# A two-layer sequence model on one core: the gates of chunks 1 to 3 a step ahead of their FFN, own orders for the first and last steps, parameters loaded first

## What is computed

```
x = layernorm(x + L0_attn(x))      # causal conv of 4 taps, gates r and i, recurrence, out projection, RMS norm
x = layernorm(x + relu(x @ W1 + b1) @ W2 + b2)
x = layernorm(x + L1_attn(x))      # selective state space, 16 states per channel
x = layernorm(x + relu(x @ w1 + b1) @ w2 + b2)

# L0_attn
xc = conv(x);  r = sigmoid(xc @ Wr.T + br);  i = sigmoid(xc @ Wi.T + bi)
a = sigmoid(log_a) ** (8 * r);  b = sqrt(clip(1 - a*a, 1e-6)) * (i * xc)
h[t] = a[t] * h[t-1] + b[t]        # with the log of the product of a clipped at -80
out = rmsnorm(h @ out_w.T) * norm_w
# L1_attn
xi, z = split(x @ in_proj.T);  xv = silu(conv(xi));  B, C, s = split(xv @ x_proj.T)
dt = softplus(s * dt_w + dt_b)
state[n][t] = exp(dt*A[n]) * state[n][t-1] + dt * B[n][t] * xv;  y = sum_n C[n][t] * state[n][t]
out = (y * silu(z)) @ out_proj.T
```

## Time and profile before

| | |
|---|---|
| median of 3 timed runs | 956.32 us (954.75 to 956.44) |
| the profiled execution, its own time | 953.83 us |
| its span in the profile | 952.0 us |
| busy: PE, DVE, ACT, POOL | 792.9, 786.3, 673.2, 586.6 us |
| mean granted clock of TensorE | 0.914 of 2.4 GHz |
| DMA | 19.49 MB, mean 20 GB/s |

### The profile page before, as it was taken

How to read it: one execution, slowest core, us unless ns; L and a number is a source line. 1 busy time by engine, 2 the same in 40 slices (tenths; PEclk the granted TensorE clock), 3 DMA queues, 4 the chain that set the end, 5 groups by cost and what they waited for, 6 DMA issues and landing times. The chain is left out here.

```text
span 952.0 us, 9608 instructions
## 1 busy us (share of the span) xinstructions
PE 792.9 (83%) x2802; PEld 530.0 (56%) x2802; DVE 786.3 (83%) x993; ACT 673.2 (71%) x1345; POOL 586.6 (62%) x488
## 2 busy tenths in 40 slices
PE   2285866988988899999999999998997797588685
PEld 2164643746565656475647564756475556356464
DVE  5425677486799999999999999999999999999750
ACT  4348687399768867997799779867976785474542
POOL 0203447448747786788678867886787577556431
PEclk9597977989998899999999999999999998799597
DMA  8100000000100010001000100010000000000000
...
DMA packets 10340, 19.49 MB, mean 20 GB/s; under 512 B 1456, under 2 KB 5296, under 8 KB 10288
## 3 DMA queue, kind: packets, MB, share of 16 engines
...
## 5 line engine op out<-in xcount | busy, mean ns | idle before, releaser
L384 POOL TENSOR_TENSOR y<-y,hC 128x1024 f32<-128x1024 f32 (+3 forms) x140 | 270.9, 1935 | 63.2 <-DVE hC L1475 58.9
L1916 PE MATMUL pC<-w,hT 128*128 128x256 f32 x1024 | 232.9, 382 | 4.4 <-ACT hT L777 4.3
L842 ACT ACTIVATE dA<-dt,A_neg 128x512 f32<-128x512 f32 (+3 forms) x320 | 185.6, 629 | 51.8 <-DVE hs L1464 51.6
L1916 PEld LDWEIGHTS pC<-w,hT 128*128 128x128 f32 x1024 | 193.5, 191 | 38.8 <-issue 6.3
L1464 DVE TENSOR_TENSOR_SCAN hs<-dA,carry,pS 128x512 f32<-128x512 f32 (+3 forms) x192 | 193.5, 1008 | 11.8 <-DVE pS L1449 4.0
L2039 PE MATMUL pS<-stack,sel 97*128 97x512 f32 (+3 forms) x320 | 151.7, 526 | 45.4 <-DVE hs L1464 45.3
L1449 DVE TENSOR_TENSOR pS<-u,pS 128x1024 f32<-128x1024 f32 (+3 forms) x160 | 159.6, 997 | 28.3 <-PE pS L2039 27.5
L1475 DVE TENSOR_TENSOR hC<-hs,pS 128x1024 f32<-128x1024 f32 (+3 forms) x160 | 158.0, 987 | 10.9 <-PE pS L2039 10.6
L1464 DVE TENSOR_TENSOR_SCAN hs<-dA,pS 128x512 f32<-128x512 f32 (+1 forms) x128 | 138.4, 1082 | 13.7 <-POOL carry L402 4.6
L777 ACT ACTIVATE hT<-pA,ffb_sb 128x512 f32<-128x512 f32 (+3 forms) x160 | 94.3, 597 | 64.0 <-PE pA L1909 63.7
L1909 PE MATMUL pA<-tg,w 128*128 128x512 f32 (+3 forms) x320 | 124.9, 538 | 5.2 <-ACT hT L777 4.8
...
## 6 DMA issues: line engine op xcount, KB each, us to landing
...
```

The costliest lines, as they stand in the source:

```text
L384: nc.gpsimd.tensor_tensor(y[:, :, 0:ch.T], so_far, hC[:, n % CRING, :, 0:ch.T], ALU.add).then_inc(S["y_sum"], 1)
L842: nc.scalar.activation(dA[:, k % ARING, 0:ch.T], dt[ch.side][:, h, 0:ch.T], ACT.Exp, scale=A_neg[:, h, n:n + 1]).then_inc(S["dA_ready"], 1)
L1916: mm = nc.tensor.matmul(dst[:, b * D:b * D + D], src(k, t0), w[:, k, :], start=k == 0, stop=k == nk - 1)
```

## The change

- **Gates ahead.** For chunks below `FIRST` = 3 the gate products go to pS's four banks (`gate_bank`), one for each product. The gate and recurrence of chunks 1, 2 and 3 are called in the step before their FFN, as the *ahead* chunk. Chunk 3's products still go to pA. The reads and writes that this brings together are kept apart by new waits: `recurrence` waits for the out product of the chunk before, `out_proj0` for the residual of the FFN before instead of `z_silu`, `in_proj_z` for `over_rms`, `x1_transpose` for z's products, `down` for `z_silu`, the first two `spread_B` for the last `gate_tanh` in pS.
- **Taps.** `EARLY` goes from 2 to 4: the taps of the first convolution of chunks 2 and 3 (512 tokens) are on VectorE.
- **Orders.** Steps 1 (`filling`), 2 (`entry`), 3 (`second`), the one with the last prep (`closing`) and the two after it (`ending`) have orders of their own; `step`, for steps 4 to 9, is as it was.
- **Start.** par is loaded first and has a semaphore of its own; ffb and rows are issued behind xt and the gate weights. Centring stands behind chunk 0's gate.

The diff, cut to what the text speaks of. Functions of one name stand once for each engine, in the order SyncE, GpSimd, ScalarE, VectorE, TensorE:

```diff
@@ -45,7 +45,9 @@
 SPLITS = ((256, 256, 512), (512, 512), (512, 512), (512, 384, 128))
 ENTRY = 2
 
-EARLY, MEARLY = 2, 1
+EARLY, MEARLY = 4, 1
+
+FIRST = 3
 LAGS = LAG_AHEAD, LAG_GATE, LAG_PREP, LAG_SCAN, LAG_TAIL = -1, 0, 1, 2, 3
 
...
@@ -192,7 +194,10 @@
         def B_bank(n):
...
+        def gate_bank(ch, w, h):
+            return pS[:, w, h, :] if ch.i < FIRST else pA[h][:]
...
-        def steps(opening, entry, step, closing):
...
+        def steps(opening, filling, entry, second, step, closing, ending):
             def chunk(i):
                 return CHUNKS[i] if 0 <= i < NCHUNK else None
...
@@ -220,11 +226,11 @@
                 ahead, gate, prep, scan, tail = (chunk(i - lag) for lag in LAGS)
                 part = step
                 if gate is None and i > 0:
-                    part = closing
+                    part = closing if prep is not None else ending
                 elif scan is None:
-                    part = opening
+                    part = opening if prep is None else filling
                 elif scan.i < ENTRY:
-                    part = entry
+                    part = entry if tail is None else second
                 part(ahead, gate, prep, scan, tail)
...
@@ -235,9 +241,7 @@
 
         @block.sync
         def _(sp):
-            for src, dst in ((par, par_sb), (ffb, ffb_sb)):
-                sp.dma_start(dst[:], src[:]).then_inc(S["small_loaded"], 16)
-            sp.dma_start(rows_sb[:], rows.rearrange("(o a) d -> o a d", o=1).to_broadcast([P, 3, D])).then_inc(S["small_loaded"], 16)
+            sp.dma_start(par_sb[:], par[:]).then_inc(S["par_loaded"], 16)
...
+                sp.dma_start(ffb_sb[:], ffb[:]).then_inc(S["small_loaded"], 16)
+                sp.dma_start(rows_sb[:], rows.rearrange("(o a) d -> o a d", o=1).to_broadcast([P, 3, D])).then_inc(S["small_loaded"], 16)
                 weight("out", out_w[:], outT)
                 weight("w1_0", w1[0][:], w1a)
                 weight("w2_0", w2[0][:], w2a)
...
@@ -366,6 +371,8 @@
             def rms_residual(ch):
                 c = ch.i
                 pool.wait_ge(S["o_scaled"], BLOCKS[c + 1])
+                if c == 0:
+                    pool.wait_ge(S["small_loaded"], 32)
...
             def entry(ahead, gate, prep, scan, tail):
-                if scan is not None:
-                    if scan.i > 0:
-                        save_carry(scan, 0)
+                row_scales(LN_PREP, prep)
+                inv_rms(gate)
+                rms_residual(gate)
+                mconv_add(prep, 1)
+                mconv_add(prep, 2)
+                mconv_add(prep, 3)
+                gate_scales(gate)
+                sum_states(scan, 4)
+                sum_states(scan, 5)
...
+            def second(ahead, gate, prep, scan, tail):
+                row_scales(LN_PREP, prep)
+                save_carry(scan, 0)
+                sum_states(tail, NS - 1)
+                save_carry(scan, 1)
+                readout(tail, gate)
...
@@ -653,7 +664,7 @@
             def par_col(h, k):
                 return par_sb[:, h, k:k + 1]
 
-            act.wait_ge(S["small_loaded"], 48)
+            act.wait_ge(S["par_loaded"], 16)
...
@@ -689,7 +700,7 @@
                 if j == 0 and ch.i > 0:
                     act.wait_ge(S["h_scan"], H * c)
                 act.wait_ge(S["gate_mm"], 4 * c + j + 1)
-                nc.scalar.activation(tg[:, j, 0:ch.T], pA[h][:, 0:ch.T], ACT.Tanh, bias=half_bias[:, h, w:w + 1],
+                nc.scalar.activation(tg[:, j, 0:ch.T], gate_bank(ch, w, h)[:, 0:ch.T], ACT.Tanh, bias=half_bias[:, h, w:w + 1],
...
@@ -1398,6 +1415,8 @@
                 c = ch.i
                 dve.wait_ge(S["d_ready"], c + 1)
                 dve.wait_ge(S["b_ready"], c + 1)
+                if c > 0:
+                    dve.wait_ge(S["out_mm"], PAIRS[c])
                 for h in range(H):
                     V.tensor_tensor_scan(st[:, H + h, 1:1 + ch.T], decay[:, h, 0:ch.T], tg[:, H + h, 0:ch.T], st[:, H + h, 0:1],
...
             def opening(ahead, gate, prep, scan, tail):
...
-                    centre_w2_0(gate)
-                if prep is not None:
...
-                if gate is not None:
                     clip_log_decay(gate)
                     log_A(gate)
                     a2_minus_1(gate)
                     gate_input(gate)
                     scaled_input(gate)
                     recurrence(gate)
-                if prep is not None:
...
+                conv_early(ahead)
                 if gate is not None:
                     row_stats(gate)
                     row_moments(gate)
...
+                    centre_b2(gate)
+                    clip_log_decay(ahead)
+                    log_A(ahead)
+                    a2_minus_1(ahead)
+                    centre_w2_0(gate)
+                    gate_input(ahead)
+                    scaled_input(ahead)
+                    recurrence(ahead)
+
+            def filling(ahead, gate, prep, scan, tail):
+                history(prep)
+                add_ffn0(prep, 0, tail)
+                centre_op(prep)
+                conv_early(ahead)
+                centre_w2_1(prep)
+                z_silu(prep, 0)
+                z_silu(prep, 1)
+                mconv_early(prep)
+                row_stats(gate)
+                mconv_silu(prep)
+                row_moments(gate)
+                x_proj_low(prep)
+                clip_log_decay(ahead)
+                log_A(ahead)
+                a2_minus_1(ahead)
+                dt_x(prep)
+                state_input(prep, 0)
+                state_scan(prep, 0, 0)
...
+                gate_input(ahead)
...
+                state_input(prep, 5)
+                scaled_input(ahead)
+                recurrence(ahead)
...
@@ -1939,19 +2040,24 @@
 
             def gate_mm(ch, w, h):
                 c = ch.i
-                if w == 0:
+                if w == 0 and h == 0:
+                    weight(ch, "gate")
+                    conv_done(pe, ch)
+                if c < FIRST:
+                    if c > 0:
+                        pe.wait_ge(S["gate_tanh"], 4 * (c - 1) + H * w + h + 1)
+                elif w == 0:
                     if h == 0:
-                        weight(ch, "gate")
-                        conv_done(pe, ch)
-                        if c > 0:
-                            pe.wait_ge(S["relu0"], FB * c)
+                        pe.wait_ge(S["relu0"], FB * c)
                 else:
                     pe.wait_ge(S["gate_tanh"], 4 * c + h + 1)
-                channel_major(ch, pA[h][:], gate_w, w * D + h * P, lambda k: conv[:, k, :], S["gate_mm"])
+                channel_major(ch, gate_bank(ch, w, h), gate_w, w * D + h * P, lambda k: conv[:, k, :], S["gate_mm"])
 
             def out_proj0(ch, prep):
                 weight(ch, "out")
-                if prep is not None:
+                if prep is not None and ch.i < FIRST:
+                    pe.wait_ge(sum_ready[LN_PREP], PAIRS[ch.i])
+                elif prep is not None:
                     pe.wait_ge(S["zz_ready"], H * (prep.i + 1))
                 pe.wait_ge(S["h_scan"], H * (ch.i + 1))
                 for j in range(ch.nj):
@@ -1965,6 +2071,8 @@
                     pe.wait_ge(S["relu1"], FB * (tail.i + 1))
                 elif h == 1 and prep is not None:
                     pe.wait_ge(S["xi_ready"], H * (prep.i + 1))
+                if h == 0 and 0 < c < FIRST:
+                    pe.wait_ge(S["z_mm"], H * c)
                 pe.wait_ge(S["gate_tanh"], 4 * c + 4)
                 pe.wait_ge(norm_ready[LN_GATE], BLOCKS[c + 1])
                 to_channel_major(ch, pA[h], x1, h, S["x1T_mm"])
@@ -1993,6 +2101,8 @@
                 centred(ch, f"w2_{layer}")
                 if layer == 0 and tail is not None:
                     pe.wait_ge(sum_ready[LN_OUT], PAIRS[tail.i + 1])
+                if layer == 0 and 0 < ch.i < FIRST:
+                    pe.wait_ge(S["zz_ready"], H * ch.i)
                 if layer == 1 and gate is not None:
                     pe.wait_ge(S["o_scaled"], BLOCKS[gate.i + 1])
                 elif layer == 1 and prep is not None:
@@ -2019,6 +2129,8 @@
                 channel_major(ch, pA[h][:], in_w, h * P, lambda k: x1T[:, k, :], S["x_mm"])
 
             def in_proj_z(ch, h, tail):
+                if ch.i + 1 < FIRST:
+                    pe.wait_ge(S["o_scaled"], BLOCKS[ch.i + 2])
 
                 if tail is not None:
                     pe.wait_ge(S["x3T_ready"], H * tail.i + h + 1)
@@ -2047,6 +2159,8 @@
                 c = ch.i
                 if n == 0:
                     pe.wait_ge(S["stack_ready"], c + 1)
+                if c == 0 and n < 2:
+                    pe.wait_ge(S["gate_tanh"], 4 * FIRST)
                 if NS * c + n >= 2:
                     pe.wait_ge(S["h_ready"], UNITS * c + H * (n - 1))
                 spread(B_bank(n), ch, n).then_inc(S["B_mm"], 1)
@@ -2076,175 +2190,180 @@
                     gate_mm(gate, 0, 1)
```

(47 more changed lines are left out.)

1568 lines of the change are left out of this document (796 added, 772 removed).

## The result

The changed kernel takes 930.66 us (median of 4 runs, 930.08 to 932.86), the kernel before 955.54 (4 runs). The ratio is 0.9752, with a 95% interval of 0.9732 to 0.9772: 2.5% faster. I had forecast 945.8 and at least 937.0. The gain is 24.9 us by the medians (23.7 by the spans of the two profiles, 952.0 and 928.3) where I had summed 10.5.

A forecast was written before the change was run, and what follows sets the result against it. VectorE was taken as full from 264 to 882 us, so gains come only before and after: -2.2 + 1.0 + 2.6 - 6.8 - 4.2 - 0.9 = -10.5 us, giving 943.3, or 945.8 as a median; range 937 to 953.

The forecast's parts named there:

- To M1: From the start to the residual of chunk 0's first FFN on VectorE: 2.2 us less, from earlier loads and later centring.
- FFN and M1 follow at the same distance: Behind chunk 0's x1 transposes: the stretch to its first FFN residual keeps its length, so 1.8 to 3.5 us are gained.
- M1 to M2: From chunk 0's first FFN residual to the first state scan: 1.0 us more, bounds -3 and +5.
- M2 to M3: From the first state scan to chunk 1's first FFN residual: 2.6 us more, bounds 0 and +5.
- M3 to M4: From chunk 1's first FFN residual to its second half of chunk 2: 6.8 us less, 70.5 us, bounds 64 and 77.
- the 2.5 us for their place: Chunk 2's FFN: 2.5 us added because chunk 3's gate products queue behind rows of states 13 to 15, tanh behind decays.
- M4 to M5: From the second half of chunk 2's FFN residual to chunk 2's second state input: 4.2 us less, bounds 0 and -9.
- The end: Last steps of the kernel: 0.9 us less, 0.7 of it from one of GpSimd's last three sums placed earlier.
- elsewhere the last two steps stay bound as they were: End of the kernel: apart from the moved sum on GpSimd, 0.7 us, the last two steps keep their bounds.
- Wider gain by the clock: Before 264 us: early gates keep TensorE busy, its clock grant rises to 0.95, 8.5 us more gain, 937; chance 0.19.
- The gain goes where it came from: Chunk 2's FFN and after: queues lose the early gate's gain to a stand, chunk 3's work merely early, 952.6; chance 0.15.
- Slower by taps and centring: Before chunk 2's second FFN residual half: VectorE becomes the bound, 12.7 us of taps and centring unhidden, 958.5; chance 0.10.

The follow-up runs named there:

- e2_loads_centre: Kernel before with the new order of parameter loads and the centring moved behind chunk 0's gate and chunk 1's taps; 948.11 us, ratio 0.9948.
- e9_old_step3: Changed kernel without chunk 3's early gate and with all of step 3 in the old order on all engines; 937.03 us, ratio 0.9817.
- e3_end: Kernel before with only the changed kernel's orders of the last three steps; 950.47 us, ratio 0.9962.
- e4_old_end: Changed kernel with the old order of the last three steps; 934.90 us, ratio 0.9815.

## Why the prediction was wrong

**The place was right, the size was not.** The full stretch only shifted: between T3 and the `dt_x` of chunk 8 it is 556.6 us after and 557.1 before. The gain comes from the two ends, as argued; I summed 10.5 us of it, and it is 24. Two of the six terms are outside their bounds: the one to M1, and the end, for which I gave none.

**To M1 (failed, -2.2 for -5.8).** The first false step was "it is issued 2.10 - 1.17 = 0.9 us earlier". I priced the issue slot; what moved was the landing that the setup of ScalarE waits for, 5.17 to 2.52, and with it the first convolution, 3.4 us. With the 3.4 for centring the bias pass of chunk 1 ended at 30.24 + 1.08 = 31.3, not at 33.8. The row that gave it away, ScalarE's wait for the third load, stood in the trace of before. Not all of this reached M1. Chunk 1's six taps now run beside GpSimd's RMS residual and took 3.60 us where I had 2.5; before they took 2.43. Timeline of VectorE, before and after:

```profile
40.79 2.43 DVE L1347 SCALAR_TENSOR_TENSOR conv<-xt,par_sb,conv 128x256 f32<-128x256 f32 x6
...
31.36 3.60 DVE L1364 SCALAR_TENSOR_TENSOR conv<-xt,par_sb,conv 128x256 f32<-128x256 f32 x6 [7.71 <-ACT conv L683]
```

TensorE waited for them and started the gate products at 35.02. The transposes started at 40.58, 4.0 us earlier than before, not the 2.2 of my sum.

The second false step was "FFN and M1 follow at the same distance". From the transposes to M1 it was 19.2 us before and is 17.3. In e2_loads_centre, without the gate products ahead of them, the transposes start at 38.18, in the changed kernel 2.4 us later, yet M1 is the same, 57.65 and 57.89. The up products behind them tell why. In e2_loads_centre, timeline of TensorE:

```profile
39.82 9.92 PE L1912 MATMUL pA<-x1T,w 128*128 128x256 f32 x32 [0.55 <-ACT x1T L770]
```

and in the changed kernel:

```profile
42.81 7.17 PE L2010 MATMUL pA<-x1T,w 128*128 128x256 f32 x32 [1.63 <-ACT x1T L780]
```

The granted clock was 0.50 to 0.57 from 38 to 46 us in the one (1.2 GHz, after a stretch of 14 us in which TensorE worked 3.8) and 1.00 from 42.8 on in the other, where the gate products had worked from 35.0. So the gate products gave back about what they took. Together the two steps make up the 3.6 us: 1.8 at the transposes and 1.9 behind them.

**M1 to M2 (+1.0 for -1.3).** Here my walk was 2.3 us too slow. The centring was hidden as I said. Up to `x_proj_low` the walk is right: VectorE gets there 21.4 us behind M1 before and 22.6 after. The difference lies between `x_proj_low` and the first decays, 7.6 us before and 4.6 after. Timelines of VectorE and ScalarE, before and after:

```profile
85.09 0.43 DVE L1431 SCALAR_TENSOR_TENSOR stack<-pA,stack 33x256 fp32r<-33x256 f32 x1 [2.38 <-ACT stack L820]
92.70 0.91 ACT L842 ACTIVATE dA<-dt,A_neg 128x256 f32<-128x256 f32 x2
...
80.48 0.43 DVE L1450 SCALAR_TENSOR_TENSOR stack<-pA,stack 33x256 fp32r<-33x256 f32 x1 [1.97 <-ACT stack L833]
85.08 0.91 ACT L855 ACTIVATE dA<-dt,A_neg 128x256 f32<-128x256 f32 x2
```

In the old order the normalisation of chunk 1 and the move of its transposes stood on ScalarE between the step sizes and the first decays; in `filling` they do not. I had no term for that. No run tests it alone, and the same stretch took 27.6 to 28.9 us in the profiles of the variants that leave it alone, so up to half of the 2.3 may be spread.

**M2 to M3, M3 to M4: numbers right.** +2.2 and -6.6 against +2.6 and -6.8. But for M3 to M4 the composition was wrong: "three more products, 5.6 us, now come in" and the 2.5 us for their place cost nothing net, as e9_old_step3 shows, and the FFN behind the transposes is 42.9 instead of 35.0 us in both kernels, for the reason that I had kept as a bound: states that VectorE delivers late. Two errors cancelled, so the good number is luck.

**M4 to M5 (-4.2 for -6.7).** I counted three products of TensorE, 5.6 us, and took 1.4 off. The early gate takes more out of step 3 than these: four tanh, two table loads and the decays of ScalarE, some 9 us of VectorE. e9_old_step3 against the changed kernel gives the size, 6.9 us from M4 to T3; which of them was the bound was not tested.

**The end (failed, -0.9 for -5.5).** I read one place on GpSimd, three sums, and wrote "elsewhere the last two steps stay bound as they were" without walking their rows. The profiles give 5.0 us to the new orders of these steps, the timed runs 3.7 in e3_end and 4.2 to 6.0 in e4_old_end; moving the sums was only one part of these orders. The other 0.5 us is the middle. Which row bounded the last two steps stays open.

**The rivals.** *Wider gain by the clock* has the right side, and what it describes happens, but at one place only: from the transposes to M1 the granted clock is 1.00 (0.81 in e2_loads_centre) and the stretch 2.2 us shorter (17.3 for 19.5). In the other stretches up to M5 the clock of before and after differs by 0.03 at most. Until M5 it is 0.87 in place of 0.86, not 0.95, so it is not the reason for the gain. *The gain goes where it came from* did not happen: it comes off in full at M5. *Slower by taps and centring*: the price was real, 6.4 us for the taps in the old order. In the changed order chunk 3's taps, though they took 9.3 us and not 3.9, and the second centring could be moved without a change in time; the changed kernel without the taps of chunks 2 and 3 was not run. The table loads kept the price of the row: in the changed kernel each takes 1.28 us and the next activation starts 0.01 to 0.02 us behind it, but where it waited for its data.

**The range** ended at 937. The two terms outside their bounds, to M1 and the end, hold 8.2 of the 13.2 us: the first rested on a wrong row, the second on no walk at all, and the range had no room for either.
